# A 16-column-head attention of a four-layer transformer kernel: another GpSimd order and layer head, and in the second such layer weights as rounded high and low parts in the values product

## The reference, cut to what matters

```python
# layer 1 (rotary, causal and padding mask); layer 2 is the same without rotary and causal mask
q = _apply_rotary(proj(query, Wq, bq), cos, sin)
k = _apply_rotary(proj(key, Wk, bk), cos, sin)
v = proj(value, Wv, bv)
scores = jnp.einsum('bhqd,bhkd->bhqk', q, k) / math.sqrt(HEAD_DIM)
scores = jnp.where(padding_mask[:, None, None, :] == 0, -1000000000.0, scores)
probs = jax.nn.softmax(scores, axis=-1)
hidden = jnp.einsum('bhqk,bhkd->bhqd', probs, v)
return hidden.transpose(0, 2, 1, 3).reshape(b, s, HIDDEN) @ Wo.T + bo
```

## Time and profile before

| | |
|---|---|
| median of 3 runs | 3799.44 us (3787.56 to 3806.21) |
| the profiled execution | 3774.63 us, its span 3772.6 us |
| PE busy | 2745.2 us, 73% of the span |
| PEld busy | 2555.8 us, 68% |
| DVE busy | 2570.8 us, 68% |
| ACT busy | 1613.3 us, 43% |
| POOL busy | 1626.4 us, 43% |
| granted TensorE clock, mean | 0.88 |

### The profile page before, as it was taken

How to read it: one execution, slowest core, us unless ns; L and a number is a source line. 1 busy time by engine, 2 the same in 40 slices (tenths; PEclk the granted TensorE clock), 3 DMA queues, 4 the chain that set the end, 5 groups by cost and what they waited for, 6 DMA issues and landing times. The chain is left out here.

```text
span 3772.6 us, 66556 instructions
## 1 busy us (share of the span) xinstructions
PE 2745.2 (73%) x20708; PEld 2555.8 (68%) x20708; DVE 2570.8 (68%) x4824; ACT 1613.3 (43%) x3415; POOL 1626.4 (43%) x1275
## 2 busy tenths in 40 slices
PE   5663584288858999739962888886289998498883
PEld 4562474288838999739961777775289888398883
DVE  4664597544437899855551998987567666388886
ACT  3222353143425555425531444443267666365551
POOL 0102455432221688730004666665344343317775
PEclk9786798599868999969975999998699999699997
DMA  3043576100035656420002555453100000365654
GB/s 97 22 135 105 191 247 187 56 18 13 7 109 186 200 195 204 158 67 18 13 4 85 157 156 155 153 155 122 55 12 6 11 11 1 129 214 178 190 180 130
DMA packets 244577, 408.83 MB, mean 108 GB/s; under 512 B 26656, under 2 KB 136492, under 8 KB 244384
## 3 DMA queue, kind: packets, MB, share of 16 engines
q1 hardware_dynamic: 230560, 368.89, 30.9%
q0 software_dynamic: 13824, 37.53, 3.0%
HBM read 327.91 MB, written 78.38 MB: 108 GB/s over the span
## 5 line engine op out<-in xcount | busy, mean ns | idle before, releaser
L500 POOL TENSOR_TENSOR moe2m_wlo<-moe2m_raw,moe2m_whi 128x768 fp32r<-128x768 f32 x184 | 342.3, 1861 | 203.2 <-ACT moe2m_whi L623 180.4
L500 POOL TENSOR_TENSOR moe1m_wlo<-moe1m_raw,moe1m_whi 128x768 fp32r<-128x768 f32 x138 | 271.8, 1975 | 157.9 <-ACT moe1m_whi L623 157.7
L717 DVE TENSOR_TENSOR moe2m_hlo<-moe2m_h_f,moe2m_hhi 128x256 fp32r<-128x256 f32 x184 | 317.1, 1723 | 13.7
L500 POOL TENSOR_TENSOR moe3m_wlo<-moe3m_raw,moe3m_whi 128x512 fp32r<-128x512 f32 x184 | 249.0, 1370 | 163.2 <-ACT moe3m_whi L623 149.9
L1889 PE MATMUL att_o<-att_vp,att_p 128*128 128x17 f32 x1792 | 239.0, 264 | 35.6 <-ACT att_p L1970 35.6
L1889 PEld LDWEIGHTS att_o<-att_vp,att_p 128*128 128x128 f32 x1792 | 234.5, 202 | 36.6 <-ACT att_p L1970 36.5
L1623 POOL TENSOR_TENSOR att_p<-att_p,att_ri 128x512 f32<-128x512 f32 x128 | 132.8, 1040 | 290.6 <-DVE att_ri L1510 289.0
L587 POOL DMA_INDIRECT rows_x<-moe_n_all,moe_slot_w x144 | 146.0, 1014 | 223.7 <-POOLq L109 121.1
L1970 ACT ACTIVATE att_p<-att_t 128x384 f32<-128x384 f32 (+1 forms) x256 | 138.2, 543 | 236.7 <-PE att_t L1865 124.1
L94 PE MATMUL moe1m_gu<-moe1m_xThi,moe1m_whi 128*128 128x256 f32 x744 | 215.7, 290 | 10.4 <-DVE moe1m_xTlo L677 8.2
L717 DVE TENSOR_TENSOR moe3m_hlo<-moe3m_act,moe3m_hhi 128x256 fp32r<-128x256 f32 x248 | 203.4, 820 | 19.3 <-issue 0.9
(11 more groups left out here) (636 smaller groups left out, 11016.6 us busy)
## 6 DMA issues: line engine op xcount, KB each, us to landing
moe1m_raw<-in_moe_w SPq DMA_DIRECT2D x186, 384.0 KB
moe2m_raw<-in_moe_w SPq DMA_DIRECT2D x184, 384.0 KB
moe3m_raw<-in_moe_w SPq DMA_DIRECT2D x248, 256.0 KB
moe0m_raw<-in_moe_w SPq DMA_DIRECT2D x92, 320.5 KB
rows_x<-att_zeros SPq DMA_DIRECT2D x24, 512.0 KB
moe0m_xr<-rows_x SPq DMA_DIRECT2D x46, 256.0 KB
rows_y<-moe0m_y SPq DMA_DIRECT2D x46, 256.0 KB, 2.4
moe1m_xr<-rows_x SPq DMA_DIRECT2D x31, 256.0 KB
```

What stands on the lines that cost most here:

```text
L500: e.tensor_tensor(wlo[s][:, :], raw[s][:, 0:WW], whi[s][:, :].bitcast(F32), ALU.subtract).then_inc(w_lo_v if in_shared(i, lo, hi, c // FC) ...
L717: v.tensor_tensor(hh[1][q][:, :], h_f[q][:, :], hh[0][q][:, :].bitcast(F32), ALU.subtract).then_inc(h_ready, 1)
```

## The change

Both layers get another layer head and another GpSimd order, and layer 2 gets a function of its own, `split_phase`, a copy of `small_phase` with the product of weights and values in two parts.

**Head and order (both layers).** The rounds nT, q and k of batch 1 move from steps -11, -10, -9 to -7, -6, -5, its qT and kT part 0 from 2 and 4 to 5 and 6, and its laying out from -2, -1 to 3, 4. SP issues the context first, then the three biases; masks, tables and the output bias are issued by ScalarE, each kind with a semaphore of its own. TensorE waits for `cleared` at step -8 and no more before its first round; the count of unmasked keys comes after the rounds k and v. The masks dg and dgc are made by GpSimd and not by VectorE. GpSimd turns q and k of batch b before norm(b + 1) and aux(b).

```diff
-    first = {"k": -12, "v": -11, "nT": -10, "q": -9}
+    own = [{("k", 0): -12, ("v", 0): -11, ("nT", 0): -10, ("q", 0): -9, ("v", 1): 1},
+           {("nT", 0): -7, ("q", 0): -6, ("k", 0): -5, ("qT", 0): 5, ("kT", 0): 6}] + [{}] * (B - 2)
-    LAY = {(16 * (b - 1) + (-2 if (kind == "q") == (b > 0) else -1)): (b, kind) for b in range(B) for kind in ("q", "k")}
+    LAY = {(16 * (b - 1) + (-2 if (kind == "q") == (b > 0) else -1) + 5 * (b == 1)): (b, kind) for b in range(B) for kind in ("q", "k")}
...
-                    pe.wait_ge(kq_done, 1)
-                    pe.wait_ge(tri_ready, 1)
-                pe.wait_ge(cleared, 1)
...
+                    if s == -8:
+                        pe.wait_ge(cleared, 1)
+                        if rotary:
+                            pe.wait_ge(tri_ready, 1)
...
                 norm(0)
+                pool.wait_ge(kq_done, 1)
+                aux(0)
+                if rotary:
+                    pool.wait_ge(tables_in, 32)
+                    turn_in(0, "k")
                 clear(0)
                 pool.drain().then_inc(cleared, 1)
-                for b in range(B):
-                    if b > 0:
-                        norm(b)
-                    if b == 0:
-                        pool.wait_ge(kq_done, 1)
-                    aux(b)
-                    for kind in ("q", "k") if rotary else ():
-                        if b > 0 or kind == "k":
-                            pool.wait_ge(f_raw, 2 * b + (kind == "k"))
-                            rotate(pool, b, kind, r1, r2).then_inc(q_ready if kind == "q" else k_ready, 1)
-                    if b == 0:
+                norm(1)
+                if rotary:
+                    for b in range(B):
+                        for t in range(TB):
+                            pool.tensor_scalar(dg[:, b, t, :], ident[:, :], kq[:, b, t:t + 1], None, ALU.mult)
+                    pool.drain()
+                    for b in range(B):
+                        pool.tensor_tensor(dgc[:, b, :], ident[:, :], dg[:, b, 0, :], ALU.subtract)
+                    pool.drain().then_inc(dg_done, 1)
+                for b in range(1, B):
+                    if rotary:
+                        turn_in(b, "q")
+                        turn_in(b, "k")
+                    if b == 1:
                         clear(1)
                         pool.drain().then_inc(cleared, 1)
+                    if b < B - 1:
+                        norm(b + 1)
+                    aux(b)
                     if b >= 2:
                         add_bias(b - 2)
```

```diff
+                def values(s):
...
+                    for i, (t, c, at) in enumerate(blocks):
+                        pe.matmul(out[:, t, g, :], p_hi[s % 4][:, at:at + P], v[:, c, h, :], start=(not rotary and g == 0 and i == 0), stop=False,
+                                  skip_group_check=True)
+                    pe.wait_ge(lo_done, s + 1)
+                    for i, (t, c, at) in enumerate(blocks):
+                        mm = pe.matmul(out[:, t, g, 0:dh + 2], p_lo[s % 4][:, at:at + P], v[:, c, h, 0:dh + 2], start=False, stop=(i == len(blocks) - 1),
+                                       skip_group_check=True)
+                    mm.then_inc(pv_done, 1)
...
+                def weights_of(s):
+                    act.wait_ge(st_ready, s + 1)
+                    if s >= 2:
+                        act.wait_ge(lo_done, s - 1)
+                    if s >= 4:
+                        act.wait_ge(pv_done, s - 3)
+                    act.activation(p_hi[s % 4][:, :], t_ps[s % 2][:, 0:QB], ACT.Exp)
+                    act.activation(p_sb[s % 2][:, :], t_ps[s % 2][:, 0:QB], ACT.Exp)
+                    act.drain().then_inc(e_done, 1)
...
+                def weights_lo(s):
+                    pool.wait_ge(e_done, s + 1)
+                    pool.tensor_tensor(p_lo[s % 4][:, :], p_sb[s % 2][:, :], p_hi[s % 4][:, :].bitcast(F32), ALU.subtract).then_inc(lo_done, 1)
...
+                for s in range(max(LAST, NS + 3)):
+                    if s < NS:
+                        weights_lo(s)
+                    if s >= 6 and (s - 6) % 4 == 0 and (s - 6) // 4 < 4 * B:
+                        add_parts((s - 6) // 4)
```

More of the change, by code:

```diff
@@ L1806, in row @@
                     sp.dma_start(dst, src.rearrange("(a d) -> a d", a=1).broadcast_to([P, D])).then_inc(loaded, 16)
-                sp.dma_start(mi[:, :], mask).then_inc(loaded, 16)
-                for q in range(3):
+                load_c(0)
+                for q in (1, 2, 0):
                     row(b3[:, q, :], biases[q])
-                row(bo[:, :], weights["bo"])
-                if rotary:
-                    sp.dma_start(cs[:, :, :, :], I["rotary"]).then_inc(loaded, 16)
-                    sp.dma_start(tri_f[:, :], I["causal"][:, 0, 0:P]).then_inc(loaded, 16)
-                load_c(0)
                 for s in range(FIRST, LAST):
@@ L2014, in _ @@
                         weights_of(s)
-                    if rotary and s == -6:
+                    if rotary and s == -2:
                         for q in range(2):
@@ L2114, in _ @@
                     v.drain().then_inc(masked, 1)
[L2115 to L2123 removed]
+                v.tensor_scalar(km[:, :], mi[:, :], 0.0, NEG, ALU.is_equal, ALU.mult)
+                v.wait_ge(loaded, 48)
+                v.tensor_scalar(b3[:, 0, :], b3[:, 0, :], scale, None, ALU.mult)
+                if not rotary:
+                    v.drain().then_inc(kq_done, 1)
                 for s in range(FIRST, max(LAST, NS + 2)):
```

568 lines of the change are left out of this document (538 added, 30 removed).

## The result

The changed kernel took 3851.66 us (median of 4 runs, 3832.54 to 3856.67), the kernel before 3793.5 us (4 runs, 3784.62 to 3806.21) in the same comparison: a ratio of 1.0141, 95% interval 1.0093 to 1.019. It is slower. The profiled execution has a span of 3846.2 us against 3772.6, and a mean granted clock of 0.848 against 0.88.

The account below looks back on a forecast made before the run. It took layer 2 as bound by TensorE, layer 1 by GpSimd's late turning. Terms -57, -16, 0, +12, +2 made -59 us: 3716 from the profiled execution, given as 3740 against the higher median; range 3708 to 3775.

Parts of the forecast that it names:

- What bounds the kernel now: Both attentions: layer 2 bound by TensorE at clock 1.00; layer 1 held by GpSimd's late turning of q and k.
- Layer 1, the order of GpSimd: Layer 1's steps: turning q and k earlier removes waits at batch boundaries; -57 us, between -65 and -45.
- Layer heads: Start of both layers: earlier transposes and first scores; -10 us in layer 1, -6 in layer 2, together -16.
- Layer 2, the product: TensorE in layer 2: eight fp32r load-and-multiply pairs a head take what eight fp32 pairs took; 0 us.
- ScalarE's lag at the boundaries: Layer 2: TensorE waits near steps 14 to 17, 2.0 us at each of six boundaries; +12 us, between 0 and 30.
- GpSimd's subtraction hides behind TensorE: Layer 2's steps: the 128x512 subtraction, taken as 1.3 us, stays under TensorE's shortest step of 1.39 us.
- Tail +2: Layer 2's end: one more exp (0.6), an unhidden subtraction (0.8) and the sum of parts (0.6); +2 us.
- the clock falls in layer 2: Rival, chance 0.04: TensorE granted 1.2 GHz over much of layer 2; all steps slow would give 3865 us.
- its mechanism: Layer 2: lighter products and small waits bring TensorE to 1.2 GHz, up to 1 us more a step.
- The argument against it: Layer 2: full stretches had clock 1.00, and their scores and projections stay, so the clock should hold.

Follow-up runs that it names:

- turn_first: The kernel before, with GpSimd turning q and k ahead of aux from batch 1 on; 3754.31 us, ratio 0.9891 to before.
- fp32_product: The changed kernel with layer 2's product as 4 fp32 matmuls of 17 columns again, low parts left out; 3850.98 us, ratio 1.0193 to before.
- double_exp: order_only with a second exp a head, into an unread tile, and the drain on ScalarE in layer 2; 3806.44 us, ratio 1.0047 to before.
- pause_late: order_only with one TensorE wait a batch in layer 2, at step 14, for the exp just sent; 3698.34 us, ratio 0.9934 to before.
- no_pool_op: one_exp_fp32 without GpSimd's operation in every step and the waits for it; ratio 0.9969 to before.
- fp32r_twice: order_only with layer 2's weights and values in fp32r, 18 columns, each head's 4 matmuls done twice; 3704.99 us, ratio 0.9952 to before.
- order_only: The changed kernel with the old function, small_phase, in layer 2; 3720.68 us, ratio 0.9826 to before.
- order_again: order_only unchanged, run again on another chip; 3658.42 us, ratio 0.9797 to before.
- one_exp_fp32: The changed kernel with one exp a head and the fp32 product of 17 columns in layer 2; ratio 0.9966 to before.
- one_exp: The changed kernel without layer 2's second exp, GpSimd's operation kept at its size; 3792.21 us, ratio 1.0018 to before.

## Why the prediction was wrong, point by point

- **What bounds the kernel now**: right for both layers. What the reading missed is how near layer 2 stood to the low clock. The earlier trace rows has the sign of it, 0.79 in a stretch where TensorE is busy 33.00 of 33 us, and a clock of 1.00 in the full batches was taken as room to spare.
- **Layer 1, the order of GpSimd** (-57, between -65 and -45): measured -61.4 (299.0 to 237.6), with a clock of 0.99, no wait of ScalarE for the turned q, and about 4.4 us from a batch's first shifted scores to its third. turn_first shows the order alone doing nearly all of it. Right.
- **Layer heads** (-16): layer 1 -8.9 for -10, the transposes 6.5 us earlier for 6. Layer 2 -0.8 for -6, with a mixture between that varies by a few microseconds, so this part stays unsure.
- **Layer 2, the product: 0.** As work this is right: 0.11 us a pair, eight pairs. **The step that failed is this one's price**, and with it that of every term of layer 2 (0, +12, +2): all were read at the granted clock of before, and the sum has nothing for a change of that clock. In its place the runs showed TensorE at 1.2 GHz over most of the layer, with a clock of 0.59 for 0.96: its busy time went from 254.5 to 385.5 us, +131, with no more matmuls. The product is not the only cause, nor needed: the fp32 product in the new function (fp32_product) runs at 0.61 too.
- **ScalarE's lag at the boundaries** (+12): the idle time of TensorE grew by 7.4 us (4.9 to 12.2), inside the bounds of 0 and 30, but not at steps 14 to 17: in the changed kernel's full batches TensorE waits at steps 4, 5 and 9. Only double_exp, where the clock is up, shows the wait for a copy of q at step 14 (0.94 us). What such a wait costs was mis-sized: pause_late loses 22 to 24 us for 4.2 us of it.
- **GpSimd's subtraction hides behind TensorE**: right. It takes 1276 ns, TensorE never waits for it, and no_pool_op gains nothing.
- **Tail +2**: right. From the last head's shifted scores to the start of the layer's last matmul it is 11.4 us (2005.21 to 2016.60) and was 9.1 (1938.13 to 1947.25). Layer 1 -61.4, heads -9.7, layer 2 +138.3 and this +2.3 make +69.5; the spans differ by 73.6, so 4.1 us are left for the mixtures.
- **The rival that came true** is the one given 0.04, *the clock falls in layer 2*, up to 3865. Of its mechanism, the runs show the small waits (pause_late) and the fp32r product (fp32r_twice) each enough alone to lose some microseconds in every batch; that the product counts because it is lighter is not shown. The argument against it, that scores and projections stay, failed. In the changed kernel's full batches four falls begin at steps 10 and 11, where no projection stands, and two at step 3, and the clock comes back between step 1 and step 7 of a batch.
- **Order of the causes.** The four batches, and the ratio less that of order_only (0.9826 and 0.9797, hence two values; the kernels ran on different chips):

| kernel | what of the new function it has | batches 2 to 5, us | over order_only, % |
|---|---|---|---|
| order_only, order_again | nothing | 136 to 137 | 0 |
| pause_late | nothing, one late pause a batch | 160 | 1.1 to 1.4 |
| fp32r_twice | the fp32r product | 164 | 1.3 to 1.6 |
| double_exp | the second exp and the drain | 164 | 2.2 to 2.5 |
| one_exp_fp32 | all but the second exp and the fp32r product | 177 | 1.4 to 1.7 |
| one_exp | all but the second exp | 162 | 1.9 to 2.2 |
| fp32_product | all but the fp32r product | 209 | 3.7 to 4.0 |
| changed kernel | all | 204 to 212 | 3.2 |

  By the ratio the second exp and the rest of the new function (one_exp_fp32) together make all of the loss, and the fp32r product, enough by itself, adds little or nothing on top. The stretches don't give that order: one_exp, with the fp32r product, has 162 us, one_exp_fp32, without it, 177. What in that rest makes its share stays open.

## What to carry to other kernels

A granted clock of 1.00 says nothing of the margin. Look in the trace of before for places where the clock falls though TensorE is busy throughout; if there are such, price a new pause or another product in the neighbouring stretches as several times itself, and give the fall a real chance. Split a change into its halves early: here one half is worth 1.7 to 2.0% and the other costs over 3%. When the sum of busy time grows with the count of instructions unchanged, read the clock by stretch before looking for waits. And compare the time of the profiled execution with the median of its kernel before a cost is read from its stretches: here one lay 39 us under.

## What the hardware showed that I had not expected

- TensorE at half clock while busy without a gap: 49.00 of 49.00 us here, 17.07 of 17.07 in fp32r_twice. The Trainium skill (TensorE: Matmul & The Clock Gate, Part 1: The HAM clock gate) says that the clock follows how busy TensorE has been lately. By the profile's busy time this trace doesn't agree; what else than busy time counts, the rows don't tell, except that a product of 64 columns is granted more (0.78 against 0.61).
- A pause of 0.94 or 1.11 us among products is followed within 0.6 us by 10 us at 1.2 GHz, one of 1.27 us ahead of projections by none.
- The same program kept layer 2 at 262 us in one profile and 295 in another, by its first and last batches.
- Between the chips, before differed by up to 2.0%, with the same ratios (0.9826 and 0.9797; 1.0141 and 1.0115).
